# Attention scores of one head per PSUM bank in three rotating banks, one exponential per head, and a fourth bank for side jobs

## The reference

```python
q = (layernorm(x) @ wq + bq).reshape(B, Sq, H, D)      # 2048 tokens
k = (y @ wk + bk).reshape(B, -1, H, D)                 # 1601 context rows
v = (y @ wv + bv).reshape(B, -1, H, D)
scores = einsum('bhqd,bhkd->bhqk', q, k) / sqrt(D)
attn = softmax(scores, axis=-1)
x = x + einsum('bhqk,bhkd->bhqd', attn, v).reshape(B, Sq, E) @ wo + bo
```

## Time and profile before

| | |
|---|---|
| runs | 4339.57 us (4332.91 to 4342.99) |
| the profiled execution | 4325.54 us, of which the span is 4323.8 us |
| PE busy | 3868.5 us, 89% |
| PE weight loads | 1740.3 us, 40% |
| DVE busy | 2605.4 us, 60% |
| ACT busy | 1964.8 us, 45% |
| max jobs, DVE reduce (L1288) | 3584, 1810.6 us |
| exponentials (L1011) | 1040 and 416 of 1024 columns, 1110 ns each |
| scores (L1865) | 3328 products, 1081.1 us |

### The profile page before, as it was taken

The page is one execution under the profiler, slowest core; times in us unless marked ns, Lnnn a source line. Parts: engine busy times, 40 slices in busy tenths (PEclk is TensorE's granted clock), DMA queues, the critical chain, the costliest instruction groups (busy, mean ns, idle before and its releaser), DMA issues. The chain is left out here.

```text
span 4323.8 us, 59344 instructions
## 1 busy us (share of the span) xinstructions
PE 3868.5 (89%) x18406; PEld 1740.3 (40%) x18407; DVE 2605.4 (60%) x5705; ACT 1964.8 (45%) x2354; POOL 402.9 (9%) x680
## 2 busy tenths in 40 slices
PE   5999999899799999966996599998989999996994
PEld 2333333556423333333664233333532333333562
DVE  4888886544598878723223465554358887874222
ACT  2667667312257767731332244444104766764110
POOL 3100000300200000023001400000211000000202
PEclk8999999899989999977998799999798999997997
DMA  7100000310100000043114100000400000002244
GB/s 129 35 9 13 11 12 2 68 34 19 38 16 13 13 10 13 2 174 116 33 32 86 59 12 16 12 8 20 74 27 27 13 10 13 11 3 70 67 145 110
DMA packets 130304, 170.30 MB, mean 39 GB/s; under 512 B 30839, under 2 KB 111935, under 8 KB 128002
## 3 DMA queue, kind: packets, MB, share of 16 engines
q1 hardware_dynamic: 118146, 126.23, 10.3%
q0 software_dynamic: 11904, 40.88, 4.2%
HBM read 114.12 MB, written 54.66 MB: 39 GB/s over the span
## 5 line engine op out<-in xcount | busy, mean ns | idle before, releaser
L1288 DVE TENSOR_REDUCE mx<-ps 128x1 f32<-128x400 f32 (+1 forms) x3584 | 1810.6, 566 | 513.9 <-PE ps L1836 511.3
L1011 ACT ACTIVATE probs<-ps,zero_col 128x1024 f32<-128x1024 f32 (+1 forms) x1040 | 1111.7, 1110 | 698.7 <-PE ps L1865 698.5
L1836 PE MATMUL ps<-k_stack,q_stack 97*128 97x400 bf16 (+1 forms) x3584 | 1111.0, 347 | 71.0 <-issue 35.8
L1865 PE MATMUL ps<-q_stack,k_stack 100*128 100x512 bf16 (+2 forms) x3328 | 1081.1, 384 | 3.8 <-ACT probs L1011 3.5
L1879 PE MATMUL ps<-probs,v 128*32 128x512 f32 (+2 forms) x5824 | 894.3, 609 | 0.2 <-ACT probs L1011 0.2
L1836 PEld LDWEIGHTS ps<-k_stack,q_stack 97*128 97x128 bf16 x3584 | 295.7, 98 | 1105.4 <-DVE mx L1288 665.3
L1011 ACT ACTIVATE probs<-ps,mask_col 128x1024 f32<-128x1024 f32 (+1 forms) x416 | 440.3, 1110 | 214.7 <-PE ps L1865 214.6
L1865 PEld LDWEIGHTS ps<-q_stack,k_stack 100*128 100x128 bf16 (+2 forms) x3328 | 325.7, 100 | 320.6 <-ACT probs L1011 56.7
L1551 DVE SCALAR_TENSOR_TENSOR x_res<-ps,comb,x_res 128x256 f32<-128x256 f32 x336 | 149.4, 483 | 162.3 <-PE ps L2055 162.2
L1879 PEld LDWEIGHTS ps<-probs,v 128*32 128x32 f32 (+2 forms) x5824 | 140.4, 112 | 244.9 <-issue 236.0
L745 POOL MEMSET wv<- 1x256 f32 x4 | 1.2, 304 | 1887.3 <-DVEq L375 1887.0
(11 more groups left out here) (250 smaller groups left out, 2835.7 us busy)
## 6 DMA issues: line engine op xcount, KB each, us to landing
q_stack<-q_parts SPq DMA_DIRECT2D x384, 64.0 KB, 2.2
q_parts<-qk_part SPq DMA_DIRECT2D x32, 384.0 KB, 2.5
w_up<-in_up SPq DMA_DIRECT2D x17, 704.0 KB, 4.2
x_place<-zeros POOLq DMA_DIRECT2D x2, 5120.0 KB, 28.8
k_stack<-k_parts SPq DMA_DIRECT2D x48, 200.1 KB, 11.9
k_stack<-k_parts POOLq DMA_DIRECT2D x48, 200.1 KB, 16.7
k_parts<-qk_part SPq DMA_DIRECT2D x24, 384.0 KB, 3.0
w_all<-in_up SPq DMA_DIRECT2D x5, 1024.0 KB, 22.3
```

The lines of the kernel that those rows point to most:

```text
L1011: act.activation(PR[pair[0] % 4][0:r, :, :], PS[0:r, 2 * b:2 * b + 2, :], ACT.Exp, bias=mask_col[0:r, k:k + 1] if L == 3 else zero_col[0:r ...
L1288: ins = dve.reduce_max(MX4[g % 2][:, u, c:c + 1], PS[:, bank, 0:CK[c]], AX.X)
L1836: last = mm(PS[:, bank, 0:CK[c]], QS[g][0:97, slot_of(j), qt * P:(qt + 1) * P], KS[0:97, (g * hpg + j) * nsub, CKO[c]:CKO[c] + CK[c]], sta ...
L1865: last = mm(PS[0:r, b + i, :], KS[0:rows, (g * hpg + jj) * nsub + sub, k * P:k * P + r], QS[g][0:rows, slot_of(jj) + sub, :], start=sub == ...
```

## The change

The scores of one head now take one bank, and banks 0, 1 and 2 are used in turn. PE may write a head when the exponential of the third head before it is done, and signals after each head. ACT makes one exponential of 512 columns per head; it still waits for a free `PR` buffer once per pair. Bank 3 becomes a fourth bank for side jobs in the iterations (not in the prologue ahead of them, where bank 3 holds projected queries), so a side job waits for DVE's job four before it. The first head of an iteration, and its first side job, wait for all earlier ones, since the counting of banks starts anew there.

```diff
+        SIDE_BANKS = [5, 6, 7, 3]
...
-                    for j in range(npair):
-                        b = pair[0] % 2
+                    for j in range(hpg):
                         sc.step()
                         act.wait_ge(s_sc, sc.at())
-                        if pv.n > 3:
-                            act.wait_ge(s_pv, pv.at(3))
-                        pv.step()
-                        act.activation(PR[pair[0] % 4][0:r, :, :], PS[0:r, 2 * b:2 * b + 2, :], ACT.Exp,
+                        if j % 2 == 0:
+                            if pv.n > 3:
+                                act.wait_ge(s_pv, pv.at(3))
+                            pv.step()
+                        act.activation(PR[head[0] // 2 % 4][0:r, j % 2, :], PS[0:r, head[0] % 3, :], ACT.Exp,
...
-                    bank = 5 + njob[0] % 3
+                    bank = SIDE_BANKS[njob[0] % banks[0]]
...
                     elif not fresh:
-                        if sf.n > 2:
-                            pe.wait_ge(s_sf, sf.at(2))
+                        pe.wait_ge(s_sf, sf.at(banks[0] - 1))
...
-                    b = 2 * (pair[0] % 2)
-                    if i == 0:
-                        if pr.n > 1:
-                            pe.wait_ge(s_pr, pr.at(1))
-                        pr.step()
+                    b = head[0] % 3
+                    head[0] += 1
+                    if head[0] == 1:
+                        if pr.n > 0:
+                            pe.wait_ge(s_pr, pr.at())
+                    elif pr.n > 2:
+                        pe.wait_ge(s_pr, pr.at(2))
+                    pr.step()
...
-                    if i == 1:
-                        pair[0] += 1
-                        last.then_inc(s_sc, 1)
+                    last.then_inc(s_sc, 1)
...
-                        use.step()
+                        use.step(2)
                         pe.wait_ge(s_pr, use.at())
```

More of the change, by code:

```diff
@@ L996, in _ @@
                                        scale=scale).then_inc(s_qe, 1)
-                pair = [0]
+                head = [0]
                 def exps(k):
                     r = key_rows(k)
-                    bias = mask_col if L == 3 else None
-                    for j in range(npair):
-                        b = pair[0] % 2
+                    for j in range(hpg):
                         sc.step()
                         act.wait_ge(s_sc, sc.at())
-                        if pv.n > 3:
-                            act.wait_ge(s_pv, pv.at(3))
-                        pv.step()
-                        act.activation(PR[pair[0] % 4][0:r, :, :], PS[0:r, 2 * b:2 * b + 2, :], ACT.Exp,
+                        if j % 2 == 0:
[3 more added lines that the diff above has]
+                        act.activation(PR[head[0] // 2 % 4][0:r, j % 2, :], PS[0:r, head[0] % 3, :], ACT.Exp,
                                        bias=mask_col[0:r, k:k + 1] if L == 3 else zero_col[0:r, :],
                                        scale=1.0).then_inc(s_pr, 1)
-                        pair[0] += 1
+                        head[0] += 1
                 def copy_sums(g):
@@ L1034, in iteration @@
                 def iteration(first):
+                    head[0] = 0
                     for g in range(NG):
@@ L1045, in _ @@
                     n = NG * NK * npair
-                    for c, per in ((sc, n), (pv, n), (o, n), (ot, NG), (rd, NG), (dv, NG)):
+                    for c, per in ((sc, 2 * n), (pv, n), (o, n), (ot, NG), (rd, NG), (dv, NG)):
                         c.loop(it, 1, per)
@@ L1270, in _ @@
                 scale = 0.25 if dh == 16 else 32.0 ** -0.5
-                njob = [0]
+                njob, banks = [0], [3]
                 nd = TPQ * hpg
                 def side(job, it):
-                    bank = 5 + njob[0] % 3
+                    bank = SIDE_BANKS[njob[0] % banks[0]]
                     njob[0] += 1
@@ L1338, in _ @@
                 per = sum(len(s) for g in range(NG) for s in side_schedule(g, hpg, False, False))
+                banks[0] = 4
                 iteration(0, True, False)
@@ L1800, in _ @@
                     ql[q].step(7 * 16)
-                njob, pair, used = [0], [0], [0]
+                njob, banks, head, used = [0], [3], [0], [0]
                 def slot_of(j):
@@ L1805, in side @@
                 def side(job):
-                    bank = 5 + njob[0] % 3
-                    fresh = njob[0] < 3
+                    bank = SIDE_BANKS[njob[0] % banks[0]]
+                    fresh = njob[0] < banks[0]
                     njob[0] += 1
@@ L1864, in scores @@
                         rows = 100 if sub == 0 else 96
-                        last = mm(PS[0:r, b + i, :], KS[0:rows, (g * hpg + jj) * nsub + sub, k * P:k * P + r],
+                        last = mm(PS[0:r, b, :], KS[0:rows, (g * hpg + jj) * nsub + sub, k * P:k * P + r],
                                   QS[g][0:rows, slot_of(jj) + sub, :], start=sub == 0, stop=sub == nsub - 1)
-                    if i == 1:
-                        pair[0] += 1
-                        last.then_inc(s_sc, 1)
+                    last.then_inc(s_sc, 1)
                 def weigh(g, k):
@@ L1925, in iteration @@
                 def iteration(first, last):
-                    njob[0] = 0
+                    njob[0] = head[0] = 0
                     for g in range(NG):
```

3 lines of the change are left out of this document (2 added, 1 removed).

## The result

The changed kernel takes 4413.6 us, the median of four runs (4402.32 to 4415.97), against 4337.65 for the kernel before (4332.91 to 4342.99, four runs): a ratio of 1.017 with a 95% interval of 1.0148 to 1.0192. Run again beside three experiments it took 4409.97 (4395.01 to 4414.43) against 4342.94: 1.0144 (1.0124 to 1.0164). It is slower by 76 us in the one set of runs and 67 in the other; 73 were forecast.

A forecast was written before the change was run, and what follows sets the result against it. PE's product stream was taken to bound the attention, with smaller waits for DVE. Losses of 40.5 us less 16.1 relief give 24.4 a layer, 73 for layers 0, 1 and 3; 4339.6 + 73 = 4413 us, range 4372 to 4440.

The forecast's parts named there:

- The chain: Head 3 reuses head 0's bank, so waits for its exponential: 1.16 us behind head 0, five-job slots lose 0.17.
- The register penalty: In the hardware loop a register instruction carries the scores' wait: 0.08 us more, five-job slots lose 0.25, six-job 0.08.
- PE's own wider register work: Four waits a slot for scores instead of two on PE: taken at nothing; 30 us in all if not covered.
- The slots with few jobs: Four-job slots lose 0.34 us each; the 16 slots without max jobs at a layer's end go from 35.5 to 40.5.
- The relief: Four side banks remove PE's waits for DVE: 16.1 us saved per four-head layer, 48 for three layers.
- Turn and out: Slots with both a turn and an out job, 3 per layer: the out job's wait for DVE shrinks, 1.1 us saved each.
- The slot after a turn: Slot where PE's loads wait for DVE's eight maxima: 3.23 to 2.83 us, 0.40 saved, 11 times per layer.
- Faster by the relief alone: Rival: head 0's exponential is read out in time, no stall, the 48 us of DVE waits go: 4292; chance 0.06.
- Near no change: Rival: register instruction costs nothing, losses half the size, 20 against 16 us per layer: 4352 and below; chance 0.07.
- No register penalty: Rival: five-job slots lose 0.17 us everywhere, in the loop too: 4388; chance 0.12.
- ACT as the bound: Rival: exponentials start 0.8 us apart without overlap, four take 3.2 a slot, some 60 us more: 4470; chance 0.06.
- The clock: Rival: PE's 0.2 us stops in nearly each slot lower the clock, two falls per iteration, 120 us: 4530; chance 0.05.

The follow-up runs named there:

- e7: Changed kernel with ACT's wait for scores written last inside the hardware loop and first outside it; 4390.52 us, 1.0114 of the kernel before.
- e3: Changed kernel with ACT's wait for the scores written last, behind the wait for a free PR buffer; 4406.36 us, 1.0147 of the kernel before.
- e5: Changed kernel with e3's order of waits and one side job instead of two ahead of head 0 in four-head layers; 4334.64 us, 0.998 of the kernel before.
- e2: Changed kernel with four score banks and three side banks, still one exponential per head; 4347.81 us, 1.0012 of the kernel before.
- e1: Changed kernel with three side banks instead of four, bank 3 left empty; 4455.57 us, 1.0261 of the kernel before.
- e10: Changed kernel with head 0's exponential cut to 256 of 512 columns from the second iteration on, four-head layers; 4322.1 us, 0.9949 of the kernel before.
- e8: Changed kernel with e7's order of waits and one side job instead of two ahead of head 0 in four-head layers; 4319.62 us, 0.9945 of the kernel before.
- e4: Changed kernel with one side job instead of two ahead of head 0 in four-head layers, the others dealt between heads; 4340.94 us, 0.9996 of the kernel before.

## Why the prediction was right, by its steps

**The chain.** Forecast: head 3 at 1.16 behind head 0 outside and 1.24 in the loop, slots of 3.00 and 3.08. Measured: 1.15 (272.23 to 273.38) and 1.23, slots of 3.00 and 3.08, in all three layers. Its terms hold one by one: 0.41 and 0.50 from head 0 to the exponential, 686 ns for it. The estimate of 0.71 us worked out from the Trainium skill (ScalarE: Activation LUTs, section "What ACT_TABLE_LOAD costs") is 0.02 too long here: the 2912 exponentials have a median of 687 ns, and the earlier trace rows of the same shape was the better source.

**The register penalty.** 0.08 was forecast from the earlier trace rows, and its removal in e7 took five-job slots in the loop from 3.08 to 3.00. I had laid it to the register instruction as such. What runs e3 and e7 show is narrower: it is where the scores' wait sits, and outside the loop the same can happen without any register (3.06 in e3). That gap in the mechanism cost nothing in the prediction and two misses in the experiments (e3, e5). PE's own wider register work, put at nothing, was nothing: 3.00 in the loop of e7 as outside, 2.83 in the loop of e2.

**The slots with few jobs.** Four-job slots 3.00 after 2.66, 0.35 against the 0.34 forecast. The 16 at the end: 41.5 after 35.5, 6.0 against 5.0. The slot of 2.49 was right (2.47); the ones in which a denominator or spread job interrupts the pattern wait too, which I had put at a bare 0.49 in all.

**The relief.** This is the term that was mis-sized, 16.1 us a layer. Of six-job slots I had taken 0.24 from one example in the loop. In the loop they went from 3.56 to 3.35, in which 0.08 is lost, so 0.29 was given; outside from 3.62 to 3.27, 0.35; the slots with an out job gave 0.34 (4.90 to 4.64 in the loop, 4.56 outside). Turn and out: 5.73 to 4.50 outside and 4.58 in the loop, 1.2 against 1.1. The slot after a turn lost its 0.40 as forecast: it is like any other. By the slots the relief is 4.4 + 11.2 + 3.7, about 19.3 us a layer. By e1 the fourth bank is worth 14.5 in layer 3, since in e1 the stall for the exponential covers part of the wait for DVE. By the experiments the losses are 36.7 (2.0 and 34.7), less than the 41.6 that the slots add up to (22.3 net of the passage and 19.3 of relief), by the same overlap.

**The sum.** 24.4 a layer was forecast; layers 0, 1 and 3 got 26.5, 20.8 and 22.2, on average 23.1, and layer 2 0.1. The spread is the passage between the loop's passes, shown above; without it they lose 21.7, 22.3 and 22.3, so the forecast of a layer was 2 us too high. The relief was 3.2 us larger than forecast and the loss at the end 1.0 larger, which makes up these 2 us. In all it is 69.4 against 73. In the 69.4 are 4.7 by the fall of the clock in layer 0, less 1.7 at the passages of layers 1 and 3; I had left such falls to the range. The 73 was so met with two errors of opposite sign in each layer and 3 us of the clock on top. That the median of the first runs is within a microsecond of the forecast is luck at this level: the second set of runs differs by 67 and not by 76.

**The rivals.** *Faster by the relief alone* would have needed an exponential of 0.52; it takes 0.69. e10, with 0.47 for head 0, is faster, at 0.9949. *Near no change* would have been losses of 20 us a layer; e1 and e2 measure 34.7 for the bank alone. *No register penalty* (4388) is what e7 built, 4390.5, and the changed kernel isn't that. *ACT as the bound*: in the timeline of a five-job slot three exponentials take 1.84 us, 0.58 from start to start, and ACT is idle 0.6 in each slot. *The clock*: it stood at 0.99 over layer 0's attention and 1.00 over the slots at its end, where PE stops for ACT in each. Inside its attentions it fell only behind the long waits at the loop's passage, once more than before. The failure mode of the Trainium skill (TensorE: Matmul & The Clock Gate, section "A second HAM failure mode: psum-queue depth-cycling"), a clock that goes up and down through short idle times of PE, didn't show in the changed kernel, though it cycles through three banks with a wait in each slot. In e3, e5, e7 and e8 single falls of 3.4 us at a layer's end, shown above, look like a trace of it, at some 1.5 us each; they are far from the 120 us of this rival. The evidence against it, was one stretch that held no such fall.

**What I didn't see.** The best answer for the same banks. I took the position of side jobs as given, and it was the lever: one job moved behind head 0 (e4) gives back the whole stall of the five-job slots outside.

## What to carry to other kernels

A PSUM bank moved from one ring to another is priced on both sides: for each ring, the work that its writer has between a write and the reuse of that bank, against the reader's latency from the write's start (here 1.16 us with an exponential of 0.69). Where the first is short by some tenths, look for independent work that can be put between before giving up on the banks: the same products in another order took this change from 1.4% slower to no difference, and 0.7% faster with two more repairs. Among waits of one instruction, see to it that the one that ends last is the one on the instruction, in each form of the code.

## What the runs showed of the hardware that I had not expected

- Where a wait is carried matters, by 0.07 to 0.09 us. The same exponential starts 0.41 us behind its head's first product with its scores' wait on it, 0.48 with the wait on a semaphore instruction ahead (e3, outside the loop), 0.50 with it on a register instruction (changed kernel, loop). Which one goes ahead differs in these kernels: the one written first in the loop, the one written last outside.
- Two waits in one slot overlap. The slot after a turn costs 0.40 by DVE alone and 0.17 by ACT alone, and with both it took 3.18 us (e1), where 3.40 was expected.
- At the passage between the loop's passes a fall of the clock costs 2 to 6 us (the three slots take 14 to 18 us, and 12 without it), and the length of PE's wait doesn't sort the cases. The clock stayed at 1.00 after 2.57 us (before, layer 0), 2.77 (e2, layer 0), 2.85 and 2.59 (e10, layers 0 and 1); it went to the lower level around waits of 2.21 and 2.38 (changed kernel, layers 1 and 3), 2.27 (e3, layer 0) and 2.83 (changed kernel, layer 0). All other kernels with three score banks have the fall in layer 0 too. What decides stays open; a comparison of two kernels by one layer can be off by this much.
- A stall of PE in each slot of 2.49 us left the granted clock at 1.00 over the slots at the end of the changed kernel's layers. With stalls of the same kind it fell for 3.4 us in one layer each of e3, e5 and e7 and in two of e8.
